# Moving step tables and layer norm products to GpSimd, halving one-hot tables, and a new order for a one-core transformer block

## The reference, cut to what matters

```
x = x + attention(layernorm(x), ctx, Wq, bq, Wk, bk)
x = x + ffn(layernorm(x), w_fc, w_proj)                 # relu, squared; weights quantised
x = x + experts(layernorm(x), fside, ctx)               # SmoothQuant int8: two linears, silu between
x = x + product_keys(layernorm(x), Wq, keys, e_down, e_up)

# weights of ffn, per block of 64, base = max(|w|) / 15:
for s in linspace(0.4, 1.0, 16):
    deq = clip(round(w / (base*s)), -15, 15) * (base*s)
    err = sum((deq - w)**2);  keep the s with the smallest err

# product keys, per token and each of 4 heads:
s1, i1 = top_k(q1 @ keys1.T, 8);  s2, i2 = top_k(q2 @ keys2.T, 8)
scores, pk = top_k(s1[:, None] + s2[None, :], 8);  idx = (i1*128 + i2)[pk]
out = sum(silu(x @ e_down[idx]) * relu(scores) * e_up[idx])
```

## Time and profile before

| | us |
|---|---|
| median of 3 runs (389.33 to 390.71) | 389.44 |
| the profiled execution's own time | 389.69 |
| its span in the profile | 387.9 |
| PE busy | 342.5 (88%) |
| DVE busy | 343.1 (88%) |
| ACT busy | 247.7 (64%) |
| POOL busy | 99.6 (26%) |

### The profile page before, as it was taken

How to read it: one execution, slowest core, us unless ns; L and a number is a source line. 1 busy time by engine, 2 the same in 40 slices (tenths; PEclk the granted TensorE clock), 3 DMA queues, 4 the chain that set the end, 5 groups by cost and what they waited for, 6 DMA issues and landing times.

```text
span 387.9 us, 8250 instructions
## 1 busy us (share of the span) xinstructions
PE 342.5 (88%) x3222; PEld 250.7 (65%) x3222; DVE 343.1 (88%) x868; ACT 247.7 (64%) x371; POOL 99.6 (26%) x148
## 2 busy tenths in 40 slices
PE   2997898598968969999979889998999999989997
PEld 2454554144423425778978767887888887778876
DVE  4999999999999999368788999999999999999940
ACT  3899999979999982227457797755766654011000
POOL 3010011340660343121001104256424158601000
PEclk9999999869999999999989999999999999999999
DMA  8930000000000007100000000000000000000000
GB/s 254 358 132 2 1 0 2 1 1 0 2 1 0 2 0 235 37 0 3 0 2 0 3 0 3 1 3 2 0 18 14 2 15 4 2 15 2 18 15 27
DMA packets 11142, 11.40 MB, mean 29 GB/s; under 512 B 608, under 2 KB 10592, under 8 KB 11104
## 3 DMA queue, kind: packets, MB, share of 16 engines
q1 hardware_dynamic: 11104, 10.88, 8.8%
HBM read 9.83 MB, written 1.05 MB: 28 GB/s over the span
## 4 chain that ended last, share of the span: by engine, by line
DVE 53%; PE 25%; ACT 10%; issue 8%; DMA 2%; SPq 1%; POOL 0%; DVEq 0%; ACTq 0%
DVE arena L1627 10%; PE pair L898 7%; PE pair L736 5%; DVE i L1966 4%; DVE arena L1617 3%; DVE s L1960 3%; DVE arena L2026 3%; PE pair L590 3%; DVE arena L2022 2%; ACT arena L1167 2%; ACT arena L1164 2%; DVE XN L1552 2%; PE pair L884 2%; DMA arena<-in_L_ffn_keys_dram 2%; DVE pk L1981 2%
## 5 line engine op out<-in xcount | busy, mean ns | idle before, releaser
L1627 DVE TENSOR_REDUCE arena<-arena 128x16 f32<-128x1024 f32 x64 | 75.8, 1207 | 0.0
L862 PE MATMUL pair<-arena,EDT 128*128 128x256 f32 x256 | 60.2, 383 | 0.0
L898 PE MATMUL pair<-EU,arena 128*128 128x256 f32 x256 | 58.4, 382 | 0.6 <-DVE arena L2050 0.6
L898 PEld LDWEIGHTS pair<-EU,arena 128*128 128x128 f32 x256 | 47.9, 190 | 7.4 <-issue 1.0
L862 PEld LDWEIGHTS pair<-arena,EDT 128*128 128x128 f32 x256 | 47.1, 190 | 6.5 <-ACT arena L1418 0.2
L608 PE MATMUL pair<-arena,WQ 128*128 128x512 fp8e4 x112 | 35.8, 403 | 13.8 <-ACT arena L1164 8.8
L620 PE MATMUL pair<-arena 128*128 128x512 fp8e4 x128 | 40.5, 399 | 2.9 <-DVE arena L1617 2.9
L452 POOL TENSOR_TENSOR arena<-arena 128x512 f32<-128x512 f32 x20 | 27.4, 1383 | 45.0 <-ACT arena L1410 45.0
L1150 ACT ACTIVATE arena<-arena,clip_bias 128x1024 fp8e4<-128x1024 f32 x32 | 37.7, 1187 | 0.3 <-PE pair L620 0.3
L1164 ACT ACTIVATE arena<-pair,sq_bias 128x1024 f32<-128x1024 f32 x32 | 36.6, 1145 | 1.3 <-PE pair L620 1.3
L1418 ACT ACTIVATE arena<-pair 128x512 f32<-128x512 f32 x32 | 19.0, 598 | 26.4 <-PE pair L862 26.4
(11 more groups left out here) (200 smaller groups left out, 642.6 us busy)
## 6 DMA issues: line engine op xcount, KB each, us to landing
arena<-in_L_ffn_e_down_dram SPq DMA_DIRECT2D x1, 2048.0 KB, 12.2
EU<-in_L_ffn_e_up_dram SPq DMA_DIRECT2D x1, 2048.0 KB, 9.3
arena<-in_L_ffn_w_fc_dram SPq DMA_DIRECT2D x2, 512.0 KB, 5.3
X<-in_x_dram SPq DMA_DIRECT2D x1, 1024.0 KB, 5.9
arena<-in_L_ffn_w_proj_dram SPq DMA_DIRECT2D x1, 1024.0 KB, 13.7
GUW<-in_fside_BxS2xS_dram SPq DMA_DIRECT2D x1, 1024.0 KB, 12.4
out_dram<-arena SPq DMA_DIRECT2D x8, 128.0 KB, 1.7
CTX<-in_ctx_dram SPq DMA_DIRECT2D x1, 512.0 KB, 4.8
```

What stands on the lines that cost most here:

```text
L862: last = pe.matmul(bk2(4 + i % 2)[:, r, :], EDT[:, k, at:at + P], xT4[:, b % 2, k, :], start=(k == 0), stop=(k == 1))
L898: last = pe.matmul(bk2(7)[:, n, :], PR[:, n, e, :], EU[:, e, :], start=(e == 0), stop=(e == EROWS - 1))
L1627: dve.tensor_reduce(err[:, g // NS % 2, :, g % NS], squares, AX.X, ALU.add).then_inc(s["reduced"], 1)
```

## The change

1. `step_tables`, `first_norm` and `second_norm` move from DVE to POOL. DVE keeps the reciprocals; a new `second_inverse(b)` does them for the second norm and signals `ln2_inv`.
2. `one_hots(t)` becomes `one_hots(t, half)`: `oh` in two instructions of 128x2048 in place of one of 128x4096, `wc` in six of 128x512 in place of one of 128x3072. A half waits only for the same half of the tile before, and `scatter` waits for its own half.
3. On POOL the squares of the ffn's second half (`square_hidden(8)` and on) wait until the last chunk is dequantised.
4. `square(g)` waits for the e_down transposes only where it reuses their buffer.
5. The lists of PE, ACT, DVE and POOL are in a new order.

```diff
+            def step_tables(k):
+
+                for j in (2 * k, 2 * k + 1):
+                    sign = -1.0 if on_act(j) else 1.0
+                    ins = pool.tensor_scalar(stepI[:, j, :], ident[:, :], sign * STEPS[j] / GRID, None, ALU.mult)
...
+            def first_norm(b):
+
+                pool.wait_ge(s["ln1_inv"], 1)
+                for t in (2 * b, 2 * b + 1):
+                    ins = pool.tensor_scalar(XN[:, t, :], X[:, t, :], mv[:, t, 0:1], rstd[:, t:t + 1],
+                                            ALU.subtract, ALU.mult)
+                ins.then_inc(s["ln1"], 1)
+
+            def second_norm(b):
+
+                pool.wait_ge(s["ln2_inv"], b + 1)
+                pool.wait_ge(s["xT_t"], B)
...
+            step_tables(0)
+            step_tables(1)
+            step_tables(2)
             scale_weights(1)
+            step_tables(3)
+            first_norm(0)
...
+            pool.wait_ge(s["wquant"], NCH)
             square_hidden(8)
...
-                if half == 0:
-                    pe.wait_ge(s["d_onehot"], t + 1)
+                pe.wait_ge(s["d_onehot"], 2 * t + half + 1)
...
-                if g > QF_LATE:
+                if g > QF_LATE and g % QDEPTH == 3:
                     act.wait_ge(s["edT_t"], EROWS // 2)
...
+            def second_inverse(b):
+
+                dve.wait_ge(s["ln2_std"], b + 1)
+                if b == 0:
+                    dve.wait_ge(s["ln1"], B)
+                dve.reciprocal(rstd[:, 2 * b:2 * b + 2], rstd[:, 2 * b:2 * b + 2]).then_inc(s["ln2_inv"], 1)
...
-            def one_hots(t):
-
+            def one_hots(t, half):
+
+                o, k = slice(NO // 2 * half, NO // 2 * half + NO // 2), slice(16 * half, 16 * half + 16)
                 if t:
-                    dve.wait_ge(s["d_c_t"], 4 * t)
-                dve.tensor_tensor(oh, iotaI.unsqueeze(1).to_broadcast([P, NO, P, NG]), over(t, 1, P), ALU.is_equal)
+                    dve.wait_ge(s["d_c_t"], 4 * t - 2 + 2 * half)
+                column = packT[:, t % 2, 1, k].rearrange("p (o g) -> p o g", g=NG).unsqueeze(2).to_broadcast(
+                    [P, NO // 2, P, NG])
+                dve.tensor_tensor(oh[:, o], iotaI.unsqueeze(1).to_broadcast([P, NO // 2, P, NG]), column, ALU.is_equal)
                 dve.wait_ge(s["d_mask"], t + 1)
...
+                for c in range(3):
+                    part = packT[:, t % 2, 2 + c, k].rearrange("p (o g) -> p o g", g=NG).unsqueeze(2).to_broadcast(
+                        [P, NO // 2, JW, NG])
+                    ins = dve.tensor_tensor(wc[:, c, o], msk[:, o], part, ALU.mult)
+                ins.then_inc(s["d_onehot"], 1)
```

More of the change, by code:

```diff
@@ L711, in _ @@
             unit(50)
-            ffn1(4)
+            ffn1(2)
             unit(51)
             unit(52)
+            ffn1(3)
             unit(53)
             unit(54)
-            ffn1(5)
+            ffn1(4)
             unit(55)
             unit(56)
+            ffn1(5)
+            unit(57)
+            unit(58)
             ffn1(6)
-            unit(57)
-            ffn1(7)
-            unit(58)
             unit(59)
@@ L727, in _ @@
             unit(62)
+            ffn1(7)
             unit(63)
@@ L904, in _ @@
             ffn1(8)
+            pe.wait_ge(s["squared"], NU)
+            pe.wait_ge(s["hsq"], 8)
+            ffn2(0, 0)
+            ffn2(1, 0)
+            w_transposed(NCH - 1)
+            gate_weights_transposed(0)
+            gate_weights_transposed(1)
+            pe.wait_ge(s["wT_e"], 8)
+            ffn2(0, 1).then_inc(s["f2_t"], 1)
+            ffn2(1, 1).then_inc(s["f2_t"], 1)
+            c_x_transposed(0)
             ffn1(9)
             ffn1(10)
-            pe.wait_ge(s["squared"], NU)
@@ L1240, in _ @@
-            square(24)
-            clip_round(31)
-            square(25)
-            absolute(2)
-            upper(2)
-            square(26)
-            square(27)
-            e_down_out(6)
-            square(28)
+            std(1, 2, "ln2")
+            square(20)
+            clip_round(25)
+            square(21)
+            clip_round(27)
+            square(22)
+            e_down_out(2)
+            square(23)
+            absolute(2)
+            e_down_out(3)
+            square(24)
@@ L1249, in _ @@
+            e_down_out(4)
+            upper(2)
+            e_down_out(5)
+            square(25)
+            std(2, 2, "ln2")
+            square(26)
+            clip_round(29)
+            std(3, 2, "ln2")
+            clip_round(31)
+            square(27)
+            clip_round(33)
+            square(28)
+            e_down_out(6)
+            square(29)
+            x1_out(0)
+            square(30)
             x1_out(1)
-            square(29)
-            square(30)
+            square(31)
@@ L1739, in _ @@
             sum_error(13)
-            add_attention(2)
-            sum_error(14)
-            add_attention(3)
-            sum_error(15)
-            second_norm(0)
-            sum_error(16)
+            clip_round(16)
+            normalise_probabilities(3)
+            sum_error(14)
+            clip_round(18)
+            sum_error(15)
+            clip_round(20)
+            sum_error(16)
+            choose(0)
+            sum_error(17)
+            add_attention(2)
             clip_round(22)
-            sum_error(17)
-            choose(0)
             sum_error(18)
@@ L1755, in _ @@
             sum_error(21)
+            sum_error(22)
+            round_quantised(0)
             clip_round(28)
-            sum_error(22)
-            second_norm(1)
             sum_error(23)
             sum_error(24)
-            round_quantised(0)
             clip_round(30)
             sum_error(25)
+            second_inverse(2)
+            clip_round(32)
             sum_error(26)
-            clip_round(32)
+            second_inverse(3)
             sum_error(27)
-            second_norm(2)
+            clip_round(34)
             sum_error(28)
-            clip_round(34)
             sum_error(29)
```

758 lines of the change are left out of this document (357 added, 401 removed).

## The result

The changed kernel takes 396.33 us (median of 4 runs, 395.22 to 396.95). Four runs of the kernel before, three of them those shown above, have a median of 390.07. The ratio is 1.0155, with a 95% interval of 1.0116 to 1.0194: 6 us slower. I had forecast 385.3, with 0.13 for slower. The profiled execution of the changed kernel took 396.95 us, its span is 395.2 (before 387.9).

What follows compares the result with a forecast made beforehand. The search was taken as bound by DVE and ACT, the second stage by PE; first stage -1.7, pairs together -1.0 and PE's waits -1.5 gave -4.2, so 389.69 became 385.5 (385.3 on the median's scale), range 380.8 to 390.8.

Steps and rivals of the forecast that it cites:

- slower: Rival, 0.13: DVE bounds 204 to 344 us, the halves cost 6.0 and GpSimd holds some; 393.4 us.
- First stage: Everything up to the second stage: search -2.6, start +1.9, end of the search -1.0, together -1.7 us.
- The end of the search: Last square to `ffn1(8)`: copies of the transposed chunk 2 follow the square directly, 1.0 us earlier.
- The start: Second attention inputs ahead of unit 0: `square(1)` at 21.3 instead of 20.46, ACT 1.9 us late.
- the search: From 20 to 140 us: work off DVE leaves ACT alone the bound, winning 2.6 of ACT's 3.4 idle us.
- Pairs 0 and 1 together: Second stage, 184 to 204 us: two pairs give PE work for its waits and slow clock, -1.0 us.
- the empty place: Two-pair stretch: PE has nothing between the first expert product and its transposes, about 2.2 us.
- What PE then waits: 204 to 344.2 us: DVE's 5 us lead less 3.0 for the halves cuts PE's waits by 1.5 us.
- DVE comes there with a lead: At 204 us: pair 1's expert layer fills a third of DVE's 15.5 idle us, 5 us.
- Halved tables: One-hot tables, second stage: six more instructions a tile, 0.5 us each tile, +3.0 us on DVE before 344.
- Holds by GpSimd: Search: DVE instructions held while POOL does the moved work, about 4 us, inside the 13.8 DVE gained.
- GpSimd holds DVE: Rival, 0.08: the work moved to POOL lengthens the search as much as it frees it; 389.5 us.

Runs made afterwards that it cites:

- e2: Old first stage joined to the changed kernel's second stage, tables in halves; 396.85 us, ratio 1.0201 to the kernel before.
- e10: Kernel before with GpSimd's 20 products of coefficients and gate done on one column alone (output not the reference's); 383.89 us, ratio 0.9849.
- e14: Kernel before with GpSimd's 20 products on one column, handed over at once, then a 128x512 product on unused memory each; 388.32 us, ratio 0.9977.
- e1: Changed kernel's first stage joined to the second stage of the kernel before, one-hot tables whole; 388.96 us, ratio 0.9985.
- e3: New first stage and two-pair block up to pair 1's second product, then the order of the kernel before, tables whole; 394.94 us, ratio 1.0125.
- e7: Changed kernel with the last ffn1 group and tiles of ffn2 moved into the two-pair block's holes in PE's list; 394.44 us, ratio 1.0094.
- e16: e3 with its two-pair block filled as in e7; 393.03 us, ratio 1.0073.
- e15: Changed kernel with e7's filling, and pair 3's integer and norm transposes moved back in PE's list; 395.26 us, ratio 1.0139.
- e5: e1 with each one-hot table replaced by its two halves, one right behind the other; 389.95 us, ratio 1.0006.
- e9: Changed kernel with GpSimd's 20 products of coefficients and gate done on one column alone (output not the reference's); 383.89 us, ratio 0.9844.
- e4: New first stage, old order up to pair 1's second product, then the changed kernel's order with tables in halves; 402.89 us, ratio 1.0364.
- e6: Changed kernel with one-hot tables in one piece again, each where its second half stood; 432.23 us, ratio 1.108.
- e11: Kernel before's start and second stage, changed kernel's search with PE's hole at its end filled by an ffn1 group; 387.99 us, ratio 0.9934.

## Why the prediction was wrong, point by point

*First stage.* -1.7 was forecast, and the pair of profiles shows -1.9 at `ffn1(8)`. That agreement is partly luck. The three other profiles with the old first stage and its unfilled end (e2, e10, e14) start `ffn1(8)` at 144.8 to 145.2, not at 146.5; the eleven with the new one start it from 143.1 to 145.0. By the medians, 145.1 and 144.3, the gain is 0.8. The end of the search is right: from the start of the last square to `ffn1(8)` it takes 3.26 us in each of the four and 2.17 in each of the eleven, 1.1 less (1.0 forecast). The start is near: `square(1)` stands at 21.73 (21.3). The term that fails is the search, -2.6. From `square(1)` to the last square it is 122.8 us in the kernel before but 121.4 in e2, e10 and e14, and 120.6 by the median of the eleven, so 0.8 against these. ACT's busy time did rise by 2.2 us in the pair of profiles, but behind the later start the last square comes no earlier (medians 141.8 and 142.1). A table takes 0.53 us on GpSimd, as forecast. What I also left out: the 1.83 us hole left at the end can throw the clock down, 1.7 us in e1.

*Pairs 0 and 1 together, -1.0.* The first failed step. I counted the two pairs as something for PE to turn to and priced the empty place at 2.2 us. PE stood 1.4, 1.1 and 1.6 us there, and ran 32 matmuls 0.9 us slower. More than that, I read the block only for PE. Bringing pair 1 along delays pair 0, and pair 0 starts the key search: its maxima came 5.5 us later, 7.4 if counted from `ffn1(8)`. e3 shows it at 5.5 to 6 us for the block alone; e7 and e16 suggest that about 2 of them are holes that other work could fill, e15's time does not bear it out.

*What PE then waits, -1.5.* The second failed step, and the larger error of reasoning. It rested on "DVE comes there with a lead" of 5 us. A lead there is none: DVE idles more than before ahead of 202, since what it has in bulk is behind pair 0's chain, not pair 1's. An engine's idle time is no store on which a later stage draws; it needs work that is ready, and the new order made it ready later.

*Halved tables, +3.0 on DVE.* Right in size by the rows (1.23 and 1.09 us for a half, some 0.4 us a tile), and a small part of the loss: 0.8 us in e5, from nothing to some 2.

*Holds by GpSimd.* I had priced these in the search, where they are hidden (5.0 us held, before 6.1), and not in the second stage, although a row of before shows one there, 2.83 us where its like took 1.75. The change moved GpSimd's weighing against DVE's list, and held time went from 8.7 to 14.2 us in a stretch where DVE is the bound. By e9 and e10 the holds cost 6.2 us more than before, a term as large as the block's. The rows had it, and the sum did not hold it.

*The rivals.* "Slower" has the right place (DVE bound from 204 on) and the wrong price: the halves, at 6.0, where e5 has about 1, and holds that I put at "some". "GpSimd holds DVE" has the right mechanism in the wrong stage.

What stays open: why one hole of 1.8 us brings the clock down in two profiles and not in nine others with the same wait; how much of the block's loss is that clock and how much the later start of the key search; and how much of e7's and e16's 2 us is filling.

## What to carry to other kernels

Before you move work so that two chains advance together, find which of them feeds the engine that bounds the next stage, and read when that engine's bulk begins. Here 5.5 of the 7.3 us lost were there by that time; e5 and e15 show that it isn't one to one. When an order is changed beside GpSimd work, count the vector engine's short instructions that will meet it: each can be held for nearly a whole GpSimd instruction (up to 1.1 us of 1.28 here), whatever its own length. And judge an order of a stage with the neighbours that it was made for: cut and joined with another it can lose more than either (e4, e6).

## What the runs showed of the hardware

The hold goes both ways. A cast on POOL that takes 0.28 us took 4.69 in e11, beside DVE's table instructions:

```profile
250.71 4.69 POOL L474 CAST i12f<-i 128x64 bf16<-128x64 uint32 x1 [7.61 <-DVE i L1982]
```

```profile
251.35 2.28 DVE L2038 TENSOR_TENSOR arena<-arena,ctxT 128x4096 bf16<-128x4096 bf16 x1
253.55 1.75 DVE L2042 TENSOR_TENSOR arena<-arena,ctxT 128x3072 bf16<-128x3072 bf16 x1
```

POOL's cast ends at 255.4, with DVE's pair of tables at 255.3. It began at 250.71, so it stood through these two and through two shorter DVE instructions ahead of them. And not all DVE instructions are held. Two products on POOL in e11, and DVE beside them:

```profile
234.57 2.53 POOL L497 TENSOR_TENSOR arena<-arena 128x512 f32<-128x512 f32 x2 [16.51 <-ACT arena L1455]
```

```profile
235.79 1.67 DVE L1976 MAX8 s<-pair 128x8 f32<-128x128 f32 x8
```

The eight maxima take 0.21 us each, as the first four do alone in e11 (0.89). They read PSUM (`pair`). Held were element-wise instructions on SBUF: shifts, clips, small scalings, one-hot pieces. That fits with the same 20 products costing the kernel before 6 us and the changed one 12: before, 13.7 of their 27.7 us lie beside maxima and index searches, in the changed kernel 2.0 of 29.2. The Trainium skill, page "SBUF — State Buffer", section "Who interferes with whom", says that the two engines share one pair of ports as an exclusive lock, for a whole instruction, and that the one that issued first has it. By that rule, the rows agree in both directions. That the cast stands through four DVE instructions is more than the rule says.

A fall of the clock can cost nearly as much again as the wait ahead of it: 1.69 us on 12 ffn1 records behind a wait of 1.83 (e1), 1.84 us on eight matmuls of the last product behind one of 2.60 (changed kernel).
